# Opening of the second attention: the second block's norm moved ahead, two gathers moved back, an early exponential

## What is computed

```python
q = (query @ Wq + bq).reshape(B, SQ, H, HD).transpose(0, 2, 1, 3)
k = (key_value @ Wk + bk).reshape(B, SK, H, HD).transpose(0, 2, 1, 3)
v = (key_value @ Wv + bv).reshape(B, SK, H, HD).transpose(0, 2, 1, 3)
scores = jnp.einsum('bhqd,bhkd->bhqk', q, k) * scale
attn = jax.nn.softmax(scores, axis=-1)
...
x = x + jnp.tanh(g_ffn[0]) * _L0_ffn_ref(_layernorm(x, axis=-1), ...)
x = x + jnp.tanh(g_xattn[1]) * _L1_xattn_ref(_layernorm(x, axis=-1), ctx_1024, ...)
```

## Time and profile before

| | |
|---|---|
| median of three executions | 1238.09 us (1234.52 to 1238.16) |
| the profiled execution, its own time | 1233.72 us |
| its span, first to last instruction | 1232.0 us |
| mean granted TensorE clock | 0.981 of 2.4 GHz |
| busy: PE, DVE, ACT, POOL | 1160.3, 990.5, 781.3, 676.2 us |
| second attention, from the first transposes of `xn` | from 602.29 us |

### The profile page before, as it was taken

How to read it: one execution, slowest core, us unless ns; L and a number is a source line. 1 busy time by engine, 2 the same in 40 slices (tenths; PEclk the granted TensorE clock), 3 DMA queues, 4 the chain that set the end, 5 groups by cost and what they waited for, 6 DMA issues and landing times.

```text
span 1232.0 us, 26547 instructions
## 1 busy us (share of the span) xinstructions
PE 1160.3 (94%) x9040; PEld 1085.2 (88%) x9041; DVE 990.5 (80%) x2045; ACT 781.3 (63%) x1489; POOL 676.2 (55%) x772
## 2 busy tenths in 40 slices
PE   6999999989889999999699999998999999899998
PEld 5999999879778999999689999997899998788887
DVE  6899999756897766666689999996987887888887
ACT  4777777668464555555377777775444546777874
POOL 5444333243105556553788777721454656788885
PEclk9999999979999999999899999999999999999999
DMA  4211121113102333333543333313000000000001
GB/s 129 56 53 53 53 57 57 46 61 112 52 1 61 109 106 109 104 105 97 130 74 66 68 67 62 62 30 103 5 2 0 0 0 1 9 18 26 26 26 35
DMA packets 70276, 68.74 MB, mean 56 GB/s; under 512 B 24576, under 2 KB 62208, under 8 KB 69952
## 3 DMA queue, kind: packets, MB, share of 16 engines
q1 hardware_dynamic: 55920, 47.77, 12.8%
q0 software_dynamic: 12576, 18.62, 8.1%
q10 hardware_dynamic: 1712, 1.50, 0.4%
HBM read 44.00 MB, written 18.61 MB: 51 GB/s over the span
## 4 chain that ended last, share of the span: by engine, by line
PE 74%; DVE 11%; ACT 5%; issue 5%; POOL 4%; DMA 1%; ACTq 0%; DVEq 0%; POOLq 0%; SPq 0%
PE PSUM L798 13%; PE PSUM L800 13%; PE PSUM L799 13%; PE PSUM L899 8%; PE PSUM L887 6%; PE PSUM L878 5%; PE PSUM L897 2%; POOL s_t_gh L2659 2%; PE PSUM L810 2%; PE PSUM L851 1%; PE PSUM L908 1%; PE PSUM L1959 1%; ACT s_m_xn L1456 1%; PE PSUM L2848 1%; PE PSUM L2849 1%
## 5 line engine op out<-in xcount | busy, mean ns | idle before, releaser
L2209 POOL TENSOR_TENSOR s_f_h_lo<-s_f_h,s_f_h_hi 128x512 fp32r<-128x512 f32 x64 | 93.4, 1466 | 102.9 <-ACT s_f_h_hi L2153 102.3
L1382 POOL DMA_INDIRECT s_m_tile_x<-normed_x,s_tokens x78 | 96.8, 1241 | 75.1 <-DVE s_tokens L1673 53.7
L899 PEld LDWEIGHTS PSUM<-s_a_v_diagonal,s_a_prob_t 128*128 128x128 f32 x1024 | 125.9, 192 | 0.0
L899 PE MATMUL PSUM<-s_a_v_diagonal,s_a_prob_t 128*128 128x36 f32 x1024 | 125.2, 268 | 0.0
L728 ACT ACTIVATE s_a_prob_t<-PSUM 128x640 f32<-128x640 f32 x128 | 90.0, 703 | 36.6 <-PE PSUM L887 34.9
L474 DVE TENSOR_REDUCE s_a_row_max<-PSUM 128x8 f32<-128x640 f32 x128 | 104.7, 818 | 7.3 <-PE PSUM L878 4.0
L481 DVE TENSOR_TENSOR s_a_less<-PSUM,s_a_row_max 128x640 f32<-128x640 f32 x128 | 104.9, 820 | 4.4
L1049 POOL DMA_INDIRECT s_x<-sorted_y,s_slots x60 | 95.3, 1588 | 19.7 <-issue 13.6
L2147 ACT ACTIVATE s_f_h<-PSUM,s_cols 128x512 f32<-128x512 f32 x64 | 44.0, 688 | 89.6 <-PE PSUM L800 89.0
L887 PE MATMUL PSUM<-s_ident,s_a_prob 128*128 128x128 f32 x640 | 93.7, 277 | 1.0
L798 PE MATMUL PSUM<-s_m_x_hi,s_m_up_w 128*128 128x256 f32 x312 | 91.8, 294 | 1.1 <-issue 1.0
(11 more groups left out here) (327 smaller groups left out, 4222.5 us busy)
## 6 DMA issues: line engine op xcount, KB each, us to landing
sorted_y<-s_m_tile_y SPq DMA_DIRECT2D x39, 256.0 KB
s_a_kd<-s_a_k_parts SPq DMA_DIRECT2D x126, 40.0 KB
s_x<-x SPq DMA_DIRECT2D x16, 256.0 KB, 3.1
s_a_ctx<-ctx SPq DMA_DIRECT2D x32, 128.0 KB, 2.8
s_moe_raw<-moe_w SPq DMA_DIRECT2D x16, 256.0 KB
normed_x<-s_m_xn SPq DMA_DIRECT2D x16, 256.0 KB, 3.1
y<-s_x SPq DMA_DIRECT2D x16, 256.0 KB, 2.1
s_late_raw<-moe_w SPq DMA_DIRECT2D x11, 256.0 KB, 2.9
```

The lines of the kernel that those rows point to most:

```text
L899: last = pe.matmul(a.o_ps[:, 2 * c:2 * c + 2, :], a.prob_t[j % 2][:, c, :], v[:, j // BT, 0, 2 * c:2 * c + 2], start=False, stop=c == PC - ...
L1382: pool.indirect_dma_start(m.tile_x[n % 2][:, t, :], None, d["normed_x"], bass.IndirectOffsetOnAxis(ap=tokens[:, BT * n + t:BT * n + t + 1] ...
L2209: pool.tensor_tensor(f.h_lo[m % 4][:], f.h[m % 4][:], f.h_hi[m % 4][:].bitcast(F32), ALU.subtract).then_inc(f.h_split, 1)
```

## The change

It has three parts, all in the second attention (`stage` 1).

- On DVE, `ln_stats(second)` and `ln_aggregate(second)` stand ahead of `q_residue(first)` and no longer behind it, and `ln_apply(second)` stands right behind `q_residue(first)`, where before it stood in the first body, behind the first `score_max` and `less_max`.
- On ACT, an exponential of one column into an unused buffer stands behind `q_rounded(first)`. The load of the exponential table, which the compiler sets ahead of the first exponential, moves with it.
- On POOL, `gather(third, 0)` moves from ahead of `add_bias(first)` to behind `inverse_std(second)`, so that it stands right ahead of `gather(third, 1)`.

```diff
--- before.py
+++ after.py
@@ -299,7 +299,7 @@
                 self.k_parts = sb(scope, n + "k_parts", [P, 2, 2, KC, CTXP], F32R)
                 self.row_max = [sb(scope, n + f"row_max{z}", [P, HPC]) for z in two]
                 self.row_sum = [sb(scope, n + f"row_sum{z}", [P, HPC, 1]) for z in two]
-                sb(scope, n + "gap", [P, 8])
+                self.unused = sb(scope, n + "gap", [P, 8])
 
                 def context_part(part, z):
                     return sb(scope, n + f"ctx_{part}{z}", [P, KC, P], F32R)
@@ -585,9 +585,10 @@
                 dve.wait_ge(f.small_in, 16)
                 bias_of_output()
                 add_rows(second)
-                q_residue(first)
                 ln_stats(second)
                 ln_aggregate(second)
+                q_residue(first)
+                ln_apply(second)
 
             def body(b, behind, ahead):
                 late_rows = a.stage == 1 and not behind
@@ -601,8 +602,6 @@
                         dve.wait_ge(gates_done, 1)
                         dve.wait_ge(a.small_in, 32)
                         bias_of_output()
-                    else:
-                        ln_apply(second)
                 if ahead:
                     x_residue(b.next())
                 score_max(b, 1)
@@ -749,6 +748,8 @@
             q_rounded(first)
             if a.stage == 0:
                 last_weights()
+            else:
+                act.activation(a.unused[:, 0:1], ones[:, 0:1], ACT.Exp)
 
             def body(b, behind, ahead):
                 if ahead:
@@ -1096,10 +1097,10 @@
                 gather(second, 0)
                 inverse_std(first)
                 gather(second, 1, a.second_rows[1])
-                gather(third, 0)
                 pool.wait_ge(mix.y_ps, SHARED + ALL)
                 add_bias(first)
                 inverse_std(second)
+                gather(third, 0)
                 gather(third, 1)
 
             def first_turn():
```

## The result

The changed kernel takes **1241.5 us** (median of 22 executions, 1236.42 to 1247.40), the kernel before on the same chips 1235.8 us (22 executions, 1233.68 to 1245.45). The ratio is **1.0051, with a 95% interval of 1.0038 to 1.0063**: slower by 0.5%, some 6 us. The time lies in the predicted range (1240.6, from 1236.0 to 1243.5), but on the side "slower by over 0.3%", to which I had given 0.19, and not on "no change". The profiled execution of after took 1242.73 us, with a span of 1241.0 and a mean granted clock of 0.975; that of before had 1232.0 and 0.981. So the two profiles differ by 9.0 us, more than the medians do.

The account below looks back on a forecast made before the run. TensorE was taken to bound the settled second attention, so the opening's delay carries to the end. 0.6 us (gathers) plus 1.9 (clock) gave 2.5 us slower: 1240.6 us against a median of 1238.1, range 1236.0 to 1243.5.

Parts of the forecast that it names:

- slower by over 0.3%: Outcome class for the whole kernel: measured time more than 0.3% above the kernel before; chance 0.19.
- no change: Outcome class for the whole kernel: time within 0.3% (3.7 us) of the kernel before; chance 0.76.
- The second block's norm: Opening, DVE: statistics and norm come earlier, so PE goes on directly behind the scores; transposes 2.06 us earlier.
- The exponential: Opening, ACT: table load covered by ScalarE's wait for PE, first exponential up to 1.28 us earlier; gain 0.
- The gathers: POOL, third block: landing of 4.0 us makes gather(third, 1) 2.9 us late and ln_apply(third) 0.6 us late.
- the slack: POOL ahead of inverse_std(third): lateness that can be absorbed, 2.26 us, or 1.69 by the row's idle time.
- The clock: PE at the third block's transposes: 3.4 us idle drops the clock, costing 1.9 us; bounds 0 and 2.9.
- The hidden landing: Rival, POOL's third-block gathers: landing in 2.9 us or less fits the slack, clock stays; 1237.3 us; chance 0.14.
- the stall without a fall of the clock: Rival, third block: gather stalls POOL but PE's clock stays up; -0.5 to +1.5 us, 1238.7; chance 0.20.
- the change does not do what it says: Rival, opening: statistics not ahead or table loaded twice, leaving the POOL part alone; +2 us and more.
- The slower side: Rival, third block: landing 4.9 us (1.5 us) plus long clock recovery (2.9 us), together 4.4, 1242.5; chance 0.14.

Follow-up runs that it names:

- experiment 1: Changed kernel with gather(third, 0) back ahead of add_bias(first), early norm and exponential kept; ratio 1.0020 against the kernel before, 1237.5 us.
- 10: experiment 1 with the third block's second rows copied to a place of their own and added by DVE; ratio 1.0028 against the kernel before, 1238.22 us.
- experiment 12: Control: kernel before with only the third block's second rows copied to a place of their own and added by DVE; ratio 1.0030, 1239.59 us.
- experiment 8: Kernel before with only the one-column exponential added behind the first queries' rounding; ratio 1.0002, 1236.29 us.
- experiment 4: Changed kernel with split_context(third) moved between the two gathers of the third block on POOL; ratio 1.0046 against the kernel before, 1241.56 us.
- experiment 5: Kernel before with extra unused products on TensorE in the idle times of the opening; ratio 1.0001, 1236.26 us.
- 7: experiment 1 with extra unused products on TensorE in the idle times of the opening; ratio 1.0025 against the kernel before, 1238.01 us.
- experiment 2: Kernel before with only gather(third, 0) moved behind inverse_std(second); ratio 1.0058, 1242.66 us.
- experiment 9: Changed kernel with the third block's second rows copied to a place of their own and added by DVE; ratio 1.0021 against the kernel before, 1238.25 us.
- experiment 3: Changed kernel with 30 unused products of 256 columns on TensorE at the end of the first block's turn; ratio 1.0044 against the kernel before, 1239.54 us.
- 6: Changed kernel with extra unused products on TensorE in the idle times of the opening; ratio 1.0045 against the kernel before, 1240.52 us.

## Why the prediction was right in its mechanism and short in its size

**The second block's norm: right.** From the first norm to the second transposes it is 611.96 - 602.81 = 9.15 us, where before has 11.59, so 2.4 us are gained (predicted 2.06), and PE goes on without a wait. Experiments 1, 10 and 12 show that the gain is real as far as the third norm, 2.3 to 2.6 us.

**The exponential: right.** Nothing; the load has its cover, and experiment 8 shows no difference.

**The gathers: right up to the last operation.** The pair starts 7.32 us behind the first norm; the prediction's 608.8 was 7.3. From the second DMA's start to the next one's start it is 616.30 - 612.19 = 4.1 us; predicted were 4.0, of which the 0.5 for the completion to reach POOL came from no row; here the packets are over at 615.7 and the next issue starts 0.6 us later. `gather(third, 1)` is 3.15 us late (13.49 instead of 10.34 from the first norm) against 2.9, and `inverse_std(third)` 0.7 us (26.22 instead of 25.53) against 0.6. The Trainium skill's rule (DMA: Bandwidth & Descriptors, section "Anatomy of one DMA — SWDGE (gpsimd) path": about 2.0 us plus the bytes over 436 GB/s, an estimate of 2.3 us here) does not hold for this adding gather: the trace shows 4.1 us, and 4.0 in experiment 4.

What the term missed is the operation itself. `s_a_var_eps` takes 0.19 us where it follows idle time (645.15) but 0.80 us at 629.03, right behind a DMA issue that lasts to 628.04 + 1.57 = 629.61: it ends 0.2 us behind that issue. So an operation listed 1.0 us behind an issue is over only at 1.8. That is another 0.6 us, and the third norm is **1.3 us** late and not 0.6, still inside my bounds of 0.5 early to 1.5 late. The prediction had both figures for the slack and took the wrong one: with the 1.69 us of idle time in the row, which begin at the issue's end, 2.9 us of lateness leave 1.2. The old place was not free by much either: there the landing takes 5.1 to 5.6 us (experiments 1, 5 and 7), and before had 5.8 us between the two issues. That the moved gather is the cause is shown: moved alone it gives the loss (experiment 2), put back it gives back 4.0 us of the median (experiment 1), and made free of the landing 3.3 (experiment 9).

**The clock: the term that was mis-sized.** I put it at 1.9 us, with 0 and 2.9 as bounds, "with 4 to 5 us of work at half speed". It did fall at the place named, but TensorE worked for 12 us at half speed, 632.2 to 644, and lost 4.6 us from the third norm to the fourth, outside those bounds. I had sized the recovery by the earlier trace rows, where the clock was still low 8 us behind the transposes of 613.09, and talked that down because much of those 8 us was idle. The row was the better guide than my discount. The profile of experiment 3 shows that the term is the clock's: with the same lateness and a short low stretch 4.1 us of it are gone. So the sum is 1.3 + 4.6 = 5.9 us instead of 0.6 + 1.9 = 2.5, against 5.7 us between the medians. That the two agree so well is in part chance: the sum is from one profiled execution of each kernel, and the executions of after are spread over 11 us.

**The time: held by luck.** The predicted difference was 2.5 us and the measured one is 5.7. The forecast of 1240.6 lies only 0.9 us from the 1241.5 measured because it was added to 1238.1, the median of three executions of the kernel before, where the 22 executions have 1235.8. From there it would have been 1238.3, with a range from 1233.7 to 1241.2, and the measured time just outside. The base was 2.3 us too high and the difference 3.2 us too small. The weights on "within 0.3%" (0.76) and "slower" (0.19) fell to the wrong side, since both missed terms push one way.

**The rivals.** The hidden landing is out (POOL waits 2.54 us), as is the stall without a fall of the clock, and "the change does not do what it says". The slower side came true in its result, though by another path: not by a landing of 4.9 us, but by the long recovery, which alone would have been enough (0.6 + 4.6 = 5.2 us).

**Where the gain went.** It was not only the gather. Experiments 1, 9 and 10 take away most of its wait and all end 0.2 to 0.3% above before. The executions' own mean clocks point to a reason. For each kernel the table has the medians over its timed executions, and the span at an equal mean clock of 0.979, read off a straight line through that kernel's executions. (For before the 86 executions beside the experiments. A thousandth of mean clock goes with 0.5 to 1.1 us in these kernels. No execution of 2 was above 0.976, so its last column is extrapolated; those of the others with 9 to 22 executions are good to about 1 us, by the scatter around the line.)

| kernel | executions | median span | median clock | span at 0.979 |
|---|---|---|---|---|
| before | 86 | 1233.8 | 0.979 | 1233.7 |
| after | 22 | 1239.8 | 0.975 | 1236.9 |
| 1, gather back | 11 | 1235.8 | 0.976 | 1234.1 |
| 2, gather alone | 6 | 1240.9 | 0.9745 | 1237.9 |
| 3, kept busy | 9 | 1237.8 | 0.979 | 1238.8 |
| 4, context between | 12 | 1239.8 | 0.9745 | 1235.1 |
| 9, own rows | 12 | 1236.5 | 0.9755 | 1232.8 |
| 10, back and own rows | 12 | 1236.4 | 0.9755 | 1234.5 |
| 12, own rows in before | 12 | 1237.8 | 0.976 | 1235.1 |
| 8, exponential | 12 | 1234.6 | 0.9785 | 1233.8 |

Of the 6 us of after, about 3 stay at an equal clock and about 3 go with the clock, where the profile alone gave the clock 4.6 of 5.9. At an equal clock, 1 is within 0.4 us of before, and 9 would be 0.9 us ahead, less than the scatter of this reckoning. So the early norm is worth at most about a microsecond, if anything, and every order but those of before and of 8 runs at a mean clock 0.003 to 0.0045 lower. This is a correlation over executions and not an experiment: a low clock while TensorE waits counts in the mean without costing time, and the mean can be raised without a gain. Experiment 3 has the mean clock of before and is still 4 us slower, and in experiments 5 to 7 useless products raised it to 0.981 to 0.983 and gained nothing. That the lower clock is what ate the gain of the early norm is thus likely and not shown.

**What stays open.** Why the clock comes back after 3.4 us in some profiles (3, 8, 10) and after 10 to 17 in others, with almost the same work on TensorE, and why it fell in experiments 1 and 9 in the wait of 0.80 us ahead of the second block's scores (and in 8 and 12 within a microsecond behind it), where the same wait left it at 1.00 in before, in after and in 10. I found no row that tells the two cases apart. The 1.5 us in the last blocks, on the other hand, need not be the change's: over the fourteen profiles that distance of the evictions runs from 17.2 us (experiment 3) to 19.1 (after), and it is 18.9 in experiment 5, which has the order of before.

## What to carry to other kernels

If a change gathers idle time of TensorE into one wait ahead of a long stretch of work, price the clock by the longest low stretch in the trace that has work in it, not by the shortest. On a queue that issues gathers in pairs that add to the same rows, the operations between the pair are what hides the landing: before moving one of them, read the time between the two starts, and follow all that is behind it to the next idle time. Forecast the difference from the kernel before, and take its time from more than three executions where they scatter as these do. And if a gain does not arrive although its waits are gone, compare the mean clocks of the executions before looking for another wait; with profiles alone, one of 1229.9 us would have passed for a success.

## What the runs showed of the hardware that was not expected

- TensorE stayed at half clock for 12 us of gapless work (after, 632.2 to 644), and in experiment 9 for 17 us in which it was idle for less than 2 (624.4 to 641.4, busy 15.19 of 17.00).
- How long a gather that adds takes to land depends on where it stands: 4.0 to 4.2 us from its start to the issue that waited for it where nothing had been issued for some microseconds ahead of its pair (after, experiments 2, 3, 4 and 6), 5.1 to 5.6 us in its old place right behind the copying gathers (experiments 1, 5 and 7), and 4.6 to 5.2 us at other places (4.91 in the earlier trace rows). The copying gather took 2.9 to 3.0 us up to `add_rows(second)` wherever VectorE waited for it (2.87 in experiment 1, where that wait is 1.00 us because VectorE was there earlier).
- A small POOL operation listed as starting while a DMA issue is still running is recorded 0.6 us longer than alone (0.80 us against 0.19), and the third norm was later by as much.
- The control of experiment 12 lost 0.3% [0.12, 0.48] by a change that moves the third norm by 0.8 us. Of the 4.0 us between the median spans, 1.4 stay at an equal mean clock; what made the clock lower no row shows.
